# Local attention on four engines: other step orders, and other places for the next stage's first steps

## The chip, the cores and the metric

The kernel runs on one core of a Trainium2 chip. The core has TensorE (PE, matmuls and transposes), VectorE (DVE), ScalarE (ACT), GpSimd (POOL) and SyncE (SP, which only issues DMAs here). The time is the device time of one execution in microseconds, the median over runs.

## What is computed

The input is a stream `x` of 4 sequences of 512 tokens with 128 features. It goes through four residual blocks. The first is a cross-attention to 77 context rows, the third a second cross-attention, the fourth a mixture of 8 experts. The second block is the one that the change touches: six layers of local attention with a feed-forward part.

```python
def attn_layer(x, Wqkv, qs, ksc, Wo):
    qkv = x @ Wqkv                       # 16 heads of 64
    q, k, v = split into heads
    q = l2norm(q) * qs;  k = l2norm(k) * ksc
    q = q * cos * scale + rotate_half(q) * sin * scale
    k = k * cos / scale + rotate_half(k) * sin / scale
    out = local_attention(q, k, v)       # windows of 32, keys of own and previous window
    return out @ Wo
def ffn_layer(x, g, bln, W1, b1, W2, b2):
    xn = layernorm(x) * g + bln
    a, gate = split(xn @ W1 + b1)
    return a * gelu(gate) @ W2 + b2
for i in range(6):
    x = attn_layer(shift_tokens(x), ...) + x
    x = ffn_layer(shift_tokens(x), ...) + x
```

## The kernel before

The stage `windowed_layers` holds the second block. Its work is cut into 24 turns (`TURNS`: 6 layers times 4 sequences, turn j is layer j // 4 of sequence j % 4) and 96 slots (`SLOTS`: slot u is tile u % 4, of 128 tokens, in turn u // 4). Everything is float32 and the instruction streams are fully unrolled.

One slot goes through these steps. PE: `project` (u, 0 to 5), one matmul each, 0 and 1 for the queries, 2 and 3 for the keys, 4 and 5 for the values, into two PSUM banks in alternation; `heads_t` (u, 0 to 3), four transposes each, which turn the normed and rotated queries (0, 1) and keys (2, 3); `scores`, 8 matmuls for the mask and 128 small ones; `probs_t` (u, 0 and 1), transposes; `pv`, 128 small matmuls; `out`, 8 matmuls (16 PE instructions with their float32 passes). ACT: squares of `project` 0 to 3 and copies of 4 and 5 into `V` (both are its `project` step), `root` (logarithm and exponential for the norms), `heads_t`, `exp`, `probs_t`, `attended`. DVE: `mul` (u, 0 to 3, the rope products, which also empty the projection bank), `norms` (sums of squares), `soft` (maximum and subtraction), `share` (sum and reciprocal), `residual`. POOL: `clamp`, `add` (the two rope products), `rope` (four small Newton operations and the scaling by the inverse norm), `weigh` (probabilities by the reciprocal).

Per turn there is the feed-forward part: PE `back`, `norm_t`, `up` (0 to 5, on the projection banks), `down`; ACT `back`, `gelu`; DVE `stats`, `scale`, `hidden`, `down`; POOL `rstd`. `enter` and `leave` bring the stream in and out of this stage. With the first slot of a layer POOL computes the rope table of the layer (`table`, L799) just ahead of the first `clamp`, and DVE's `mul` waits for it. SP copies V shifted by 32 rows for each slot: after `v_done` of `project` 4 the lower half (L755), after that of `project` 5 and the landing of the lower half the upper one (L758); then, for u below 68, it fills a part of `sorted_rows` in HBM for a later stage (L777), and ahead of the next slot it copies the 32 rows that wrap (L752).

What runs when is written out by hand in four lists, `PE_TURN`, `ACT_TURN`, `DVE_TURN` and `POOL_TURN`: the steps of one turn, with the slot relative to the turn (-2 to 7) and the step's number. `steps` repeats a list for j from -2 to TURNS + 2 and leaves out slots that do not exist, so an engine's list may begin anywhere in the cycle; only the cyclic order counts. Each engine executes its list in order, with semaphore waits on the others. A step's PSUM bank for the shared kinds is dealt out in PE's order, in a ring of four (`homes`). The dictionary `FIRST` hangs the next stage's first steps (`f_...`, a part of the second cross-attention for the first sequence) behind named steps near the end.

Of the kernel before, what the change touches and what calls it, by code (L numbers as in the profile page):

```python
# [2479 lines left out]
```

## Time and profile before

| | us |
|---|---|
| median of 3 runs | 2054.53 |
| lowest and highest | 2050.99, 2066.19 |
| the profiled execution | 2048.87 |
| its span, first to last instruction | 2047.1 |
| mean granted clock of PE, share of full | 0.958 |

The stage of the change fills the span from about 113 to 1806 us, the first cross-attention stands ahead of it and the rest of the second one with the experts behind it. Durations below are of the one profiled execution; so a sum that is made from them is made against its 2048.87 us. In a group's row of the page "busy" is the union of its instructions, the mean is of one of them, and behind the bar stands the idle time of the engine just before them with what ended it. PE is the matmul queue, PEld the weight loads beside it; each PE instruction counted in the program is one load and one matmul.

### The profile page before, as it was taken

The page shows a single profiled execution, that of the slowest core. Times are in us where ns is not written, and L with a number is a line of the kernel's source. Part 1 is how long each engine was busy: PE and PEld are TensorE (multiplying, and loading weights), DVE is VectorE, ACT ScalarE, POOL GpSimd, SP SyncE. Part 2 cuts the span into 40 slices and gives each one's busy share as a digit, 9 for nine tenths or more (in the row PEclk, how much of TensorE's full clock was granted, in tenths as well). Part 3 has the DMA queues.
Part 4 walks back from the last instruction along what each step waited for, and adds up shares of the span by engine and source line. Part 5 has one row for each costly group of instructions (what it writes and reads, how often), then busy time and mean ns, then how long its engine had stood idle before and what let it go on. Part 6 is the DMA issues. An engine that isn't in the chain of part 4 may idle for free. (4 is left out here: it accounts for less than half of the span.)

```text
span 2047.1 us, 78950 instructions
## 1 busy us (share of the span) xinstructions
PE 1850.1 (90%) x32837; PEld 1300.6 (64%) x32837; DVE 1440.9 (70%) x2605; ACT 1135.4 (55%) x2379; POOL 1435.4 (70%) x1838
## 2 busy tenths in 40 slices
PE   4769999999999999999999989999999999789858
PEld 3636666666666666666666656666666676556648
DVE  2357778777777777787778867778777787445546
ACT  1135665566566566665566656566656665434425
POOL 1168888778888788788778877888778887412334
PEclk9779999999999999999999999999999999889969
DMA  3021131111311113111113111121111111030012
GB/s 98 0 40 50 47 96 55 42 43 49 101 47 43 49 47 94 50 49 47 46 47 100 51 43 44 34 82 35 27 34 31 37 31 33 10 95 1 22 34 69
DMA packets 60836, 99.93 MB, mean 49 GB/s; under 512 B 15847, under 2 KB 35064, under 8 KB 58642
## 3 DMA queue, kind: packets, MB, share of 16 engines
q1 hardware_dynamic: 58978, 91.72, 15.5%
q8 instruction: 262, 4.29, 0.9%
q0 software_dynamic: 1504, 3.17, 0.5%
q14 instruction: 92, 0.75, 0.1%
HBM read 44.50 MB, written 21.45 MB: 32 GB/s over the span
## 5 line engine op out<-in xcount | busy, mean ns | idle before, releaser
L1273 PE MATMUL b_bank_proj<-layer_weights,b_stream_t 128*128 128x512 f32 x1152 | 616.9, 635 | 21.0 <-DVE b_plain_moved L1069 17.5
L1069 DVE TENSOR_TENSOR b_plain_moved<-b_bank_proj,b_rope 128x1024 f32<-128x1024 f32 x384 | 468.9, 1222 | 210.3 <-ACT b_squares L903 179.2
L812 POOL TENSOR_TENSOR b_rotated<-b_plain_moved 128x1024 f32<-128x1024 f32 x192 | 452.5, 2357 | 42.6 <-DVE b_plain_moved L1069 42.6
L827 POOL TENSOR_TENSOR b_rotated<-b_rotated,b_inv_norm 128x1024 f32<-128x1024 f32 x192 | 365.2, 1902 | 15.4
L903 ACT ACTIVATE b_squares<-b_bank_proj 128x512 f32<-128x512 f32 x384 | 229.6, 598 | 110.2 <-PE b_bank_proj L1273 107.6
L832 POOL TENSOR_TENSOR b_probs<-b_probs,b_inv_sum 128x512 f32<-128x512 f32 x192 | 200.3, 1044 | 81.7 <-DVE b_inv_sum L1090 81.7
L1281 PEld LDWEIGHTS b_bank_shared<-const_tables,b_rotated 128*128 128x128 f32 x1536 | 187.7, 145 | 109.7 <-issue 103.5
L1273 PEld LDWEIGHTS b_bank_proj<-layer_weights,b_stream_t 128*128 128x128 f32 x1152 | 187.8, 195 | 108.7 <-issue 58.5
L1075 DVE TENSOR_REDUCE b_norm<-b_squares 128x16 f32<-128x1024 f32 x192 | 232.2, 1209 | 1.0 <-issue 0.2
L910 ACT ACTIVATE b_v<-b_bank_proj 128x512 f32<-128x512 f32 x192 | 114.5, 596 | 194.3 <-PE b_bank_proj L1273 194.3
L1281 PE MATMUL b_bank_shared<-const_tables,b_rotated 128*128 128x128 f32 x1536 | 210.8, 279 | 2.5 <-POOL b_rotated L827 2.4
L940 ACT ACTIVATE b_attended_t<-b_bank_shared 128x512 f32<-128x512 f32 x192 | 109.5, 596 | 168.5 <-PE b_bank_shared L1335 168.5
L1347 PEld LDWEIGHTS b_bank_shared<-b_attended_t,layer_weights 128*128 128x128 f32 x1536 | 184.5, 193 | 26.6 <-issue 25.8
L1347 PE MATMUL b_bank_shared<-b_attended_t,layer_weights 128*128 128x128 f32 x1536 | 188.3, 276 | 1.6 <-ACT b_attended_t L940 1.6
L1081 DVE TENSOR_REDUCE b_max<-b_bank_scores 128x8 f32<-128x512 f32 x192 | 131.6, 685 | 62.6 <-PE b_bank_scores L1306 62.2
L1306 PE MATMUL b_bank_scores<-b_k_t,b_q_t 64*32 64x64 f32 x12288 | 148.4, 225 | 27.6 <-issue 26.4
L1306 PEld LDWEIGHTS b_bank_scores<-b_k_t,b_q_t 64*32 64x32 f32 x12288 | 141.4, 105 | 38.4 <-issue 31.6
L924 ACT ACTIVATE b_k_t<-b_bank_shared 128x512 f32<-128x512 f32 x192 | 106.4, 594 | 91.4 <-PE b_bank_shared L1281 91.4
L1316 PEld LDWEIGHTS b_bank_shared<-const_tables,b_probs 128*128 128x128 f32 x768 | 95.2, 141 | 87.4 <-issue 86.8
L1335 PE MATMUL b_bank_shared<-b_probs_t,b_v 64*64 64x32 f32 x6144 | 118.5, 222 | 33.4 <-issue 33.1
L1378 PE MATMUL b_bank_proj<-b_normed_t,layer_weights 128*128 128x512 f32 (+1 forms) x288 | 141.3, 600 | 0.5 <-DVE b_normed_t L1119 0.5
L1087 DVE TENSOR_REDUCE b_sum<-b_probs 128x8 f32<-128x512 f32 x192 | 128.9, 671 | 15.5 <-ACT b_probs L930 15.3
(346 smaller groups left out, 2920.9 us busy)
## 6 DMA issues: line engine op xcount, KB each, us to landing
b_v_shifted<-b_v SPq DMA_DIRECT2D x192, 192.0 KB, 2.4
sorted_rows<-sorted_rows SPq DMA_DIRECT2D x66, 258.0 KB
layer_weights<-L_ffn_Wqkv SPq DMA_DIRECT2D x6, 1536.0 KB
b_v_shifted<-b_v SPq DMA_DIRECT2D x72, 128.0 KB, 3.1
layer_weights<-L_ffn_Wo SPq DMA_DIRECT2D x6, 512.0 KB
c_sorted_in<-sorted_rows SPq DMA_DIRECT2D x23, 129.0 KB, 2.0
layer_weights<-L_ffn_w SPq DMA_DIRECT2D x8, 256.0 KB, 6.1
c_w<-L_ffn_w SPq DMA_DIRECT2D x8, 256.0 KB, 5.9
```

Of the source, the lines that this page charges most:

```text
L812: nc.gpsimd.tensor_tensor(out=turned[:, k, :], in0=pm[:, k, 0, :], in1=pm[:, k, 1, :], op=ALU.add).then_inc(add_done, 1)
L827: nc.gpsimd.tensor_tensor(out=tk, in0=tk, in1=repeat_last(rn[:, k, :], DH), op=ALU.mult).then_inc(rope_done, 1)
L832: nc.gpsimd.tensor_tensor(out=p, in0=p, in1=repeat_last(share[:, b, :], LOOK), op=ALU.mult).then_inc(p_done, 1)
L903: nc.scalar.activation(squares[:, (c % 2) * 512:(c % 2) * 512 + 512], bk_proj[c % 2][:, :], ACT.Square).then_inc(sq_done, 1)
L1069: nc.vector.tensor_tensor(to, src.to_broadcast(shape), tab.to_broadcast(shape), ALU.mult).then_inc(mul_done, 1)
L1075: nc.vector.tensor_reduce(ss[:, k, :], squares[:, :].rearrange("p (a h c) -> p h a c", a=2, h=HEADS), AX.XY, ALU.add).then_inc(ss_done, 1)
L1081: nc.vector.tensor_reduce(top[:, b, :], s, AX.X, ALU.max).then_inc(max_done, 1)
L1273: nc.tensor.matmul(out, xs[:, b, t * P:(t + 1) * P], w, start=True, stop=True).then_inc(proj_full, 1)
L1281: last = nc.tensor.transpose(bank[:, n * P:(n + 1) * P], turned[:, g // 2, at:at + P], ident)
L1306: last = nc.tensor.matmul(bk_s[r][to, at:at + LOOK], qT[rows, u % 2, p, w, :], kT[rows, p, t * P + w * WIN:t * P + w * WIN + LOOK], start= ...
L1347: last = nc.tensor.matmul(bank[:, 0:P], weights(l, W_O + n * P, P), OT[:, u % 2, n, :], start=(n == 0), stop=(n == PAIRS - 1))
L1378: nc.tensor.matmul(bk_proj[c % 2][0:w, :], weights(l, W_UP + at, w), xnT[:, :], start=True, stop=True).then_inc(up_full, 1)
```

## The change

Only the four lists and `FIRST` change. Every list holds the same steps per turn as before, with a few of them counted from another turn (for example `leave` at -2 in place of -3), and in another order. In the cyclic order of PE: before, `down(-2)` stood behind `pv(-2)`, after it stands ahead of it; `probs_t(-1, 0)` moves ahead of `scores(0)`; `out(-2)` from ahead of `scores(0)` to behind `probs_t(-1, 1)`; `scores(1)` from behind `back(-1)` to ahead of it; `scores(2)` from behind the first four `up` to behind the first; `scores(3)` (written -1 before) from the middle of the projections of slot 4 to behind the last `up`; `heads_t(4, 0)` and `(4, 1)` (written 0) from behind `project(5, 0)` to ahead of `project(4, 5)`; `heads_t(3, 0)` and `(3, 1)` from behind `project(4, 2)` to ahead of it. On DVE `norms(4, 0)` goes ahead of `mul(4, 0)` (in the other slots it mostly keeps its place or moves by one), `soft` and `residual` steps move by a few places. On POOL `clamp`, `add` and `weigh` change places around the `rope` steps. On ACT `exp`, `attended`, `root` and `heads_t` steps move.

In `FIRST`, `f_weights` on PE goes from behind the last `out` to behind the last `back`; on DVE `f_stream` moves up behind a `share`, `f_normed` goes from behind the last `scale` to behind the last `stats`, `f_own` behind the second last `hidden`; on POOL `f_fill` and `f_rstd` hang behind `weigh` steps.

The lists of PE, DVE and POOL, and `FIRST`:

```diff
 PE_TURN = [
-    ("project", 0, 3), ("scores", -1, 0), ("project", 0, 4), ("probs_t", -2, 0), ("project", 0, 5), ("leave", -3, 0),
-    ("probs_t", -2, 1), ("project", 1, 0), ("heads_t", 0, 0), ("project", 1, 1), ("enter", 1, 0), ("heads_t", 0, 1),
-    ("pv", -2, 0), ("project", 1, 2), ("down", -2, 0), ("heads_t", 0, 2), ("heads_t", 0, 3), ("project", 1, 3),
-    ("project", 1, 4), ("out", -2, 0), ("scores", 0, 0), ("project", 1, 5), ("probs_t", -1, 0), ("project", 2, 0),
-    ("probs_t", -1, 1), ("project", 2, 1), ("heads_t", 1, 0), ("heads_t", 1, 1), ("pv", -1, 0), ("project", 2, 2),
-    ("project", 2, 3), ("out", -1, 0), ("heads_t", 1, 2), ("heads_t", 1, 3), ("project", 2, 4), ("back", -1, 0),
-    ("probs_t", 0, 0), ("scores", 1, 0), ("project", 2, 5), ("project", 3, 0), ("probs_t", 0, 1), ("project", 3, 1),
-    ("pv", 0, 0), ("project", 3, 2), ("heads_t", 2, 0), ("heads_t", 2, 1), ("project", 3, 3), ("norm_t", -1, 0),
-    ("out", 0, 0), ("up", -1, 0), ("heads_t", 2, 2), ("heads_t", 2, 3), ("up", -1, 1), ("probs_t", 1, 0),
-    ("up", -1, 2), ("up", -1, 3), ("scores", 2, 0), ("project", 3, 4), ("project", 3, 5), ("probs_t", 1, 1),
-    ("project", 4, 0), ("project", 4, 1), ("pv", 1, 0), ("project", 4, 2), ("heads_t", 3, 0), ("heads_t", 3, 1),
-    ("out", 1, 0), ("up", -1, 4), ("up", -1, 5), ("heads_t", 3, 2), ("heads_t", 3, 3),
+    ("heads_t", 0, 0), ("heads_t", 0, 1), ("project", 0, 5), ("probs_t", -2, 1), ("project", 1, 0), ("project", 1, 1),
+    ("down", -2, 0), ("project", 1, 2), ("pv", -2, 0), ("project", 1, 3), ("heads_t", 0, 2), ("heads_t", 0, 3),
+    ("probs_t", -1, 0), ("project", 1, 4), ("scores", 0, 0), ("project", 1, 5), ("heads_t", 1, 0), ("project", 2, 0),
+    ("project", 2, 1), ("heads_t", 1, 1), ("probs_t", -1, 1), ("out", -2, 0), ("project", 2, 2), ("enter", 1, 0),
+    ("pv", -1, 0), ("project", 2, 3), ("heads_t", 1, 2), ("heads_t", 1, 3), ("out", -1, 0), ("scores", 1, 0),
+    ("back", -1, 0), ("project", 2, 4), ("project", 2, 5), ("probs_t", 0, 0), ("probs_t", 0, 1), ("heads_t", 2, 0),
+    ("project", 3, 0), ("heads_t", 2, 1), ("project", 3, 1), ("pv", 0, 0), ("project", 3, 2), ("norm_t", -1, 0),
+    ("project", 3, 3), ("out", 0, 0), ("heads_t", 2, 2), ("heads_t", 2, 3), ("up", -1, 0), ("scores", 2, 0),
+    ("up", -1, 1), ("up", -1, 2), ("up", -1, 3), ("probs_t", 1, 0), ("project", 3, 4), ("project", 3, 5),
+    ("probs_t", 1, 1), ("project", 4, 0), ("project", 4, 1), ("pv", 1, 0), ("heads_t", 3, 0), ("heads_t", 3, 1),
+    ("project", 4, 2), ("out", 1, 0), ("heads_t", 3, 2), ("heads_t", 3, 3), ("up", -1, 4), ("up", -1, 5),
+    ("leave", -2, 0), ("scores", 3, 0), ("project", 4, 3), ("project", 4, 4), ("probs_t", 2, 0),
 ]
...
 DVE_TURN = [
-    ("soft", 2, 1), ("mul", 4, 0), ("norms", 4, 0), ("mul", 4, 1), ("mul", 4, 2), ("share", 2, 0), ("hidden", -1, 1),
-    ("hidden", -1, 2), ("share", 2, 1), ("residual", 1, 0), ("mul", 4, 3), ("norms", 4, 1), ("soft", 3, 0),
-    ("soft", 3, 1), ("mul", 5, 0), ("share", 3, 0), ("mul", 5, 1), ("norms", 5, 0), ("share", 3, 1), ("mul", 5, 2),
-    ("down", -1, 0), ("mul", 5, 3), ("norms", 5, 1), ("residual", 2, 0), ("soft", 4, 0), ("soft", 4, 1),
-    ("mul", 6, 0), ("mul", 6, 1), ("norms", 6, 0), ("share", 4, 0), ("share", 4, 1), ("mul", 6, 2),
-    ("residual", 3, 0), ("norms", 6, 1), ("mul", 6, 3), ("stats", 0, 0), ("soft", 5, 0), ("mul", 7, 0), ("mul", 7, 1),
-    ("norms", 7, 0), ("soft", 5, 1), ("mul", 7, 2), ("scale", 0, 0), ("share", 5, 0), ("mul", 7, 3), ("share", 5, 1),
-    ("norms", 7, 1), ("residual", 4, 0), ("hidden", 0, 0), ("soft", 6, 0),
+    ("share", 1, 0), ("mul", 3, 2), ("scale", -1, 0), ("mul", 3, 3), ("share", 1, 1), ("norms", 3, 1),
+    ("residual", 0, 0), ("hidden", -1, 0), ("soft", 2, 0), ("soft", 2, 1), ("norms", 4, 0), ("mul", 4, 0),
+    ("share", 2, 0), ("mul", 4, 1), ("mul", 4, 2), ("share", 2, 1), ("residual", 1, 0), ("hidden", -1, 1),
+    ("hidden", -1, 2), ("soft", 3, 0), ("mul", 4, 3), ("norms", 4, 1), ("share", 3, 0), ("soft", 3, 1), ("mul", 5, 0),
+    ("norms", 5, 0), ("mul", 5, 1), ("down", -1, 0), ("mul", 5, 2), ("share", 3, 1), ("mul", 5, 3), ("norms", 5, 1),
+    ("soft", 4, 0), ("soft", 4, 1), ("mul", 6, 0), ("norms", 6, 0), ("mul", 6, 1), ("share", 4, 0),
+    ("residual", 2, 0), ("mul", 6, 2), ("share", 4, 1), ("mul", 6, 3), ("norms", 6, 1), ("residual", 3, 0),
+    ("soft", 5, 0), ("stats", 0, 0), ("soft", 5, 1), ("mul", 7, 0), ("mul", 7, 1), ("norms", 7, 0),
 ]
...
 POOL_TURN = [
-    ("add", -1, 0), ("weigh", -3, 1), ("clamp", -1, 1), ("rope", -1, 0), ("add", -1, 1), ("clamp", 0, 0),
-    ("rope", -1, 1), ("add", 0, 0), ("weigh", -2, 0), ("weigh", -2, 1), ("rope", 0, 0), ("clamp", 0, 1),
-    ("add", 0, 1), ("rope", 0, 1), ("add", 1, 0), ("clamp", 1, 0), ("weigh", -1, 0), ("rope", 1, 0), ("weigh", -1, 1),
-    ("clamp", 1, 1), ("add", 1, 1), ("rope", 1, 1), ("add", 2, 0), ("clamp", 2, 0), ("weigh", 0, 0), ("rope", 2, 0),
-    ("clamp", 2, 1), ("weigh", 0, 1), ("add", 2, 1), ("rstd", -1, 0), ("clamp", 3, 0), ("rope", 2, 1),
-    ("weigh", 1, 0),
+    ("clamp", 5, 0), ("add", 5, 0), ("rope", 5, 0), ("weigh", 3, 1), ("clamp", 5, 1), ("add", 5, 1), ("rope", 5, 1),
+    ("clamp", 6, 0), ("add", 6, 0), ("weigh", 4, 0), ("rope", 6, 0), ("weigh", 4, 1), ("add", 6, 1), ("clamp", 6, 1),
+    ("rstd", 0, 0), ("rope", 6, 1), ("clamp", 7, 0), ("add", 7, 0), ("weigh", 5, 0), ("weigh", 5, 1), ("clamp", 7, 1),
+    ("rope", 7, 0), ("add", 7, 1), ("clamp", 8, 0), ("rope", 7, 1), ("weigh", 6, 0), ("add", 8, 0), ("rope", 8, 0),
+    ("weigh", 6, 1), ("add", 8, 1), ("clamp", 8, 1), ("weigh", 7, 0), ("rope", 8, 1),
 ]
...
 FIRST = {
-    "pe": {("out", SLOTS - 1, 0): ("f_weights",), ("norm_t", TURNS - 1, 0): ("f_contexts",),
+    "pe": {("back", TURNS - 1, 0): ("f_weights",), ("norm_t", TURNS - 1, 0): ("f_contexts",),
             ("up", TURNS - 1, 1): ("f_normed", "f_keys",), ("up", TURNS - 1, 3): ("f_queries",),
             ("up", TURNS - 1, 5): ("f_scores", "leave",), ("down", TURNS - 1, 0): ("f_counts",)},
     "act": {("back", TURNS - 1, 0): ("f_weights", "f_contexts",), ("gelu", TURNS - 1, 0): ("f_normed",),
             ("gelu", TURNS - 1, 2): ("f_keys", "f_queries", "f_scores", "leave", "f_counts",)},
-    "dve": {("residual", SLOTS - 2, 0): ("f_stream",), ("scale", TURNS - 1, 0): ("f_normed", "f_own",),
+    "dve": {("share", SLOTS - 2, 0): ("f_stream",), ("stats", TURNS - 1, 0): ("f_normed",), ("hidden", TURNS - 1, 1): ("f_own",),
             ("hidden", TURNS - 1, 2): ("f_best",), ("down", TURNS - 1, 0): ("f_counts",)},
-    "pool": {("rope", SLOTS - 4, 1): ("f_fill",), ("rstd", TURNS - 1, 0): ("f_rstd",)},
+    "pool": {("weigh", SLOTS - 6, 1): ("f_fill",), ("weigh", SLOTS - 2, 0): ("f_rstd",)},
 }
```

The list of ACT (80 steps) is left out. In its new order `project`, `heads_t` and `probs_t` keep the sequence that PE's new order gives them nearly throughout, with `exp(3, 1)` (written -1) behind `root(5, 0)` and the two `attended` of a slot close together.

## Rows read from the trace of the kernel before

**Rows 1.** The page of the profile: busy time of the engines; two DMA kinds; one issue.

```profile
PE 1850.1 (90%) x32837; PEld 1300.6 (64%) x32837; DVE 1440.9 (70%) x2605; ACT 1135.4 (55%) x2379; POOL 1435.4 (70%) x1838
...
q8 instruction: 262, 4.29, 0.9%
...
b_v_shifted<-b_v SPq DMA_DIRECT2D x192, 192.0 KB, 2.4
```

**Rows 2.** Windows, a turn without and one with a new layer: us, busy by engine, PEclk, DMA share, GB/s.

```profile
1119.40:1186.40 67.00, 63.95 (x1291) 43.95 (x1290) 53.26 (x79) 41.84 (x86) 56.55 (x71) 1.00 0.17 48
1186.40:1258.40 72.00, 65.74 (x1292) 45.02 (x1291) 53.31 (x79) 41.85 (x86) 57.62 (x74) 0.98 0.16 45
```

**Rows 3.** Waits over the whole span: engine, line, releaser: us in total, times, longest.

```profile
PE b_bank_shared L1335 <- issue: 39.4, 33, 2.1
...
PE b_bank_scores L1306 <- issue: 26.4, 32, 1.5
...
DVE b_plain_moved L1069 <- POOL b_rope L799: 23.9, 6, 5.3
```

**Rows 4.** Timeline of PE, turn of a new layer: start us, duration us, instructions.

```profile
1186.87 1.95 PE L1347 MATMUL b_bank_shared<-b_attended_t,layer_weights 128*128 128x128 f32 x16
1188.66 1.02 PE L1378 MATMUL b_bank_proj<-b_normed_t,layer_weights 128*128 128x512 f32 x2
1189.52 1.04 PE L1281 MATMUL b_bank_shared<-const_tables,b_rotated 128*128 128x128 f32 x8
...
1193.50 0.41 PE L1296 MATMUL b_bank_scores<-b_mask_bands,b_mask_rows 64*32 64x512 bf16 x8
...
1195.12 1.99 PE L1273 MATMUL b_bank_proj<-layer_weights,b_stream_t 128*128 128x512 f32 x4
```

**Rows 5.** Timeline, all engines, the first slot of a new layer.

```profile
1198.89 2.79 POOL L799 TENSOR_TENSOR b_rope<-const_tables,b_qk_scale 128x256 f32<-128x256 f32 x4
1199.19 1.13 PE L1335 MATMUL b_bank_shared<-b_probs_t,b_v_shifted 64*64 64x32 f32 x64
...
1202.99 2.07 PE L1273 MATMUL b_bank_proj<-layer_weights,b_stream_t 128*128 128x512 f32 x2 [1.73 <-DVE b_plain_moved L1069]
...
1204.35 0.22 POOL L817 TENSOR_TENSOR b_newton_half<-b_inv_norm_first 128x16 f32<-128x16 f32 x1
...
1205.54 1.90 POOL L827 TENSOR_TENSOR b_rotated<-b_rotated,b_inv_norm 128x1024 f32<-128x1024 f32 x1
```

**Rows 6.** The page, costliest groups: busy us, mean ns of one | idle before.

```profile
L1069 DVE TENSOR_TENSOR b_plain_moved<-b_bank_proj,b_rope 128x1024 f32<-128x1024 f32 x384 | 468.9, 1222 | 210.3 <-ACT b_squares L903 179.2
L812 POOL TENSOR_TENSOR b_rotated<-b_plain_moved 128x1024 f32<-128x1024 f32 x192 | 452.5, 2357 | 42.6 <-DVE b_plain_moved L1069 42.6
L827 POOL TENSOR_TENSOR b_rotated<-b_rotated,b_inv_norm 128x1024 f32<-128x1024 f32 x192 | 365.2, 1902 | 15.4
L903 ACT ACTIVATE b_squares<-b_bank_proj 128x512 f32<-128x512 f32 x384 | 229.6, 598 | 110.2 <-PE b_bank_proj L1273 107.6
L832 POOL TENSOR_TENSOR b_probs<-b_probs,b_inv_sum 128x512 f32<-128x512 f32 x192 | 200.3, 1044 | 81.7 <-DVE b_inv_sum L1090 81.7
...
L1075 DVE TENSOR_REDUCE b_norm<-b_squares 128x16 f32<-128x1024 f32 x192 | 232.2, 1209 | 1.0 <-issue 0.2
```

**Rows 7.** Timeline of PE, a gap inside a `scores` step.

```profile
1009.88 0.68 PE L1306 MATMUL b_bank_scores<-b_k_t,b_q_t 64*32 64x64 f32 x43 [1.05 <-issue]
```

**Rows 8.** Timeline, PE and the SP queue, a gap inside the `pv` step after `scores(1)`.

```profile
975.20 0.51 SPq L758 DMA_DIRECT2D b_v_shifted<-b_v  x1
...
976.74 1.14 PE L1335 MATMUL b_bank_shared<-b_probs_t,b_v_shifted 64*64 64x32 f32 x64
...
977.64 0.54 SPq L777 DMA_DIRECT2D sorted_rows<-sorted_rows  x1
...
980.31 0.81 PE L1335 MATMUL b_bank_shared<-b_probs_t,b_v 64*64 64x32 f32 x41 [2.09 <-issue]
```

**Rows 9.** Windows, the same stretch: us, busy by engine, PEclk, DMA share, GB/s.

```profile
976.20:977.40 1.20, 1.17 (x47) 0.69 (x48) 1.20 (x1) 0.98 (x3) 1.20 (x3) 1.00 0.57 164
```

More of the change, by code:

```diff
@@ L513 @@
-    ("exp", 0, 1), ("attended", -1, 0), ("attended", -1, 1), ("project", 2, 2), ("heads_t", 1, 1), ("root", 2, 0),
-    ("project", 2, 3), ("heads_t", 1, 2), ("heads_t", 1, 3), ("back", -1, 0), ("project", 2, 4), ("probs_t", 0, 0),
-    ("project", 2, 5), ("project", 3, 0), ("probs_t", 0, 1), ("project", 3, 1), ("root", 2, 1), ("attended", 0, 0),
-    ("exp", 1, 0), ("project", 3, 2), ("attended", 0, 1), ("project", 3, 3), ("exp", 1, 1), ("root", 3, 0),
-    ("heads_t", 2, 0), ("heads_t", 2, 1), ("gelu", -1, 0), ("gelu", -1, 1), ("heads_t", 2, 2), ("heads_t", 2, 3),
@@ L518 @@
-    ("gelu", -1, 2), ("probs_t", 1, 0), ("project", 3, 4), ("project", 3, 5), ("probs_t", 1, 1), ("project", 4, 0),
-    ("root", 3, 1), ("project", 4, 1), ("attended", 1, 0), ("attended", 1, 1), ("project", 4, 2), ("heads_t", 3, 0),
+    ("heads_t", 0, 1), ("probs_t", -2, 1), ("project", 1, 2), ("root", 1, 0), ("exp", -1, 1), ("attended", -2, 0),
+    ("project", 1, 3), ("heads_t", 0, 2), ("heads_t", 0, 3), ("project", 1, 4), ("attended", -2, 1),
+    ("probs_t", -1, 0), ("project", 1, 5), ("root", 1, 1), ("project", 2, 0), ("exp", 0, 0), ("project", 2, 1),
@@ new lines @@
+    ("heads_t", 1, 0), ("heads_t", 1, 1), ("probs_t", -1, 1), ("exp", 0, 1), ("root", 2, 0), ("project", 2, 2),
+    ("attended", -1, 0), ("attended", -1, 1), ("enter", 1, 0), ("project", 2, 3), ("heads_t", 1, 2),
+    ("heads_t", 1, 3), ("back", -1, 0), ("project", 2, 4), ("project", 2, 5), ("probs_t", 0, 0), ("exp", 1, 0),
+    ("probs_t", 0, 1), ("project", 3, 0), ("project", 3, 1), ("heads_t", 2, 0), ("root", 2, 1), ("heads_t", 2, 1),
+    ("attended", 0, 0), ("attended", 0, 1), ("project", 3, 2), ("project", 3, 3), ("exp", 1, 1), ("root", 3, 0),
@@ new lines @@
+    ("heads_t", 2, 2), ("heads_t", 2, 3), ("gelu", -1, 0), ("gelu", -1, 1), ("gelu", -1, 2), ("probs_t", 1, 0),
+    ("project", 3, 4), ("project", 3, 5), ("probs_t", 1, 1), ("root", 3, 1), ("project", 4, 0), ("project", 4, 1),
+    ("exp", 2, 0), ("exp", 2, 1), ("attended", 1, 0), ("attended", 1, 1), ("root", 4, 0), ("project", 4, 2),
+    ("heads_t", 3, 0), ("heads_t", 3, 1), ("heads_t", 3, 2), ("heads_t", 3, 3), ("project", 4, 3), ("project", 4, 4),
+    ("exp", 3, 0), ("leave", -2, 0), ("heads_t", 4, 0), ("probs_t", 2, 0), ("project", 4, 5), ("project", 5, 0),
@@ L520 @@
+    ("root", 4, 1), ("project", 5, 1),
 ]
 DVE_TURN = [
-    ("soft", 2, 1), ("mul", 4, 0), ("norms", 4, 0), ("mul", 4, 1), ("mul", 4, 2), ("share", 2, 0), ("hidden", -1, 1),
-    ("hidden", -1, 2), ("share", 2, 1), ("residual", 1, 0), ("mul", 4, 3), ("norms", 4, 1), ("soft", 3, 0),
-    ("soft", 3, 1), ("mul", 5, 0), ("share", 3, 0), ("mul", 5, 1), ("norms", 5, 0), ("share", 3, 1), ("mul", 5, 2),
-    ("down", -1, 0), ("mul", 5, 3), ("norms", 5, 1), ("residual", 2, 0), ("soft", 4, 0), ("soft", 4, 1),
```

6 lines of the change are left out of this document (removed).

## Prediction

> **What bounds the kernel.** I read the page first: TensorE (PE) is busy 1850.1 us, VectorE (DVE) 1440.9, GpSimd (POOL) 1435.4, ScalarE 1135.4 [rows 1]. Then windows cut at `norm_t`, one for each turn of the stage. A turn without a new layer lasts 67.0 us, with PE busy 63.95 and POOL 56.55; a turn in which a layer begins lasts 72.0, with PE at 65.74 and a lower granted clock [rows 2]. The change permutes the same steps, so PE's work stays and only what lies between its steps can move. The waits say what that is: 39.4 us inside `pv` and 26.4 inside `scores`, both "issue" (PE waits for nothing that the profile shows), and 23.9 us of DVE waiting for the rope table [rows 3].
>
> The "issue" gaps are instruction supply. The instruction queue moved 4.29 MB in 262 packets, 16.4 KB each; PE ran 2 x 32837 instructions and about a thousand waits, so a packet is some 256 of them [rows 1]. A `scores` step is 272 PE instructions in 1.62 us (1195.12 - 1193.50) [rows 4], a `pv` step 256 and a few waits in 3.80 - 1.73 = 2.07 us [rows 5]. Elsewhere PE is slow per instruction: `out` takes 32 in 1.79 us, a 512-wide projection 2 in some 0.9 (the `up` of rows 4 shows 0.86). So a block lasts long everywhere but in those two steps. They stop for 1.05 us [rows 7], and once for 2.09 [rows 8].
>
> **The change, part by part.** No step is added or removed. PE's step times without gaps, from rows 4 and 5: `project` and `up` 0.87, `heads_t` and `probs_t` 0.44, `scores` 1.62, `pv` 2.0, `out` 1.79, `down` 2.6 (three chunks of two `up`-sized matmuls).
>
> *A, start of a layer (5 times in the steady part).* Before: `project(4,0)`, `(4,1)`, `pv`, `project(4,2)`. POOL ends the table at 1201.68; DVE can only then do `mul(4,0)` (1.22 us), which empties the bank of `project(4,2)`; PE stands 1.73 us and then runs two matmuls in 2.07 where 1.02 is usual for the shape [rows 4, 5]. After: two `heads_t` (0.87) stand ahead of `project(4,2)`, and on DVE `norms(4,0)` goes ahead of `mul(4,0)`, filling the table's wait. If POOL starts the table as late as now, `mul(4,0)` ends 3.75 us after the `pv` begins and PE wants it at 2.9: the gap falls to about 0.87, 5 x 0.87 = 4.3 us. The slow clock behind it costs 1.05 us on that pair and some 0.6 on what follows; if three of five such spells go, 3 x 1.6 = 4.8. A is -9. Bounds: -4 (gap alone), -17 (gap and clock loss gone, 5 x 3.3).
>
> *B, tighter chains in every turn.* `norms` before `mul(4,0)` makes the bank of `project(4,2)` free 0.60 + 1.21 + 1.22 + some 0.1 = 3.15 us after `project(4,1)` [rows 6]; PE arrives after 2.0 + 0.87 = 2.88. That is 0.27 us a turn, hidden when PE stands in the `pv` between. Then `heads_t(4,0)`: behind `project(4,1)` stand on POOL the clamp, `rope(3,1)` (small steps 1205.54 - 1204.35 = 1.19, then 1.90), `weigh(2,0)` 1.04, `add(4,0)` 2.36, `rope(4,0)` 3.09 [rows 5, 6]; with the square 0.60, `norms` 1.21 and hand-overs that is 11.8 us. PE gets there after `pv`, 2 `heads_t`, `project`, `out`, 2 `heads_t`, 2 `up`, `scores`, 2 `project`, `probs_t` = 11.9 us. It is hidden by 0.1 us only. POOL is busy 56.55 of 67 us [rows 2], so its queue is nowhere far behind; what waits behind `rope(4,0)` is `weigh`, `add(4,1)`, `rope(4,1)`, whose reader `heads_t(4,2)` has 3 us to spare. Before, `project(4,1)` to `heads_t(4,0)` took 14.1 us by the same step times. The other shortened leads (`project(5,1)` to `heads_t(5,0)`, 15.4 to 11.0 us) have at least 1.6 us left by the same sum. I take +3 over 23 turns; bounds 0 (PE's own gaps cover it) and +12 (0.5 us a turn).
>
> *C, instruction supply.* Each fast step is as long as a block, so each holds about one block boundary in either order: 65 gaps in 192 fast steps [rows 3] stay about 65. What can change is their length. Before, `scores(1)` and `pv(0)` are 3.05 us apart, `scores(2)` and `pv(1)` 3.9, the others 4.3 or more; after, `pv(-2)` and `scores(0)` are 3.05 apart, `pv(-1)` and `scores(1)` 3.5, the others 5.7 or more. About even. The 2.09 us gap has one more thing in it: SyncE issued the upper half of V's shifted copy at 975.20, the DMA engines were 0.57 busy from 976.20 to 977.40, and `pv` began at 976.74 [rows 8, 9]; I read the gap as a block whose transfer stood behind V's. In the new order that copy still meets `pv(0)`: its lower half is issued by `project(2,4)`, 4.35 us ahead, and the upper one after its landing 2.4 us later [rows 1]. And `pv(-2)` and `pv(-1)`, 5.65 us behind `project(0,5)` and `project(1,5)` now, meet the next transfer, the filling of `sorted_rows` (L777), issued when V's copy has landed; this copy ends after 68 of the 96 slots, 17 turns. At a third of 34 steps (33 `pv` gaps in 96 [rows 3]) and 2.09 - 1.05 = 1.04 us, that is +12; my times for those transfers are good to half a microsecond, so I count half, +6, and -4 for the pairs moved apart. C is +2. Bounds: -18 (every gap in `pv` at 0.6 us in place of 1.2) and +22 (all collisions, and a spell of slow clock of 1.6 us behind six of them).
>
> *D, ends of the stage.* `f_weights` moves behind `back(23)`, `f_normed` ahead of `scale(23)`, `f_stream` and `f_rstd` earlier: all of it fills waits of the last turn's serial chain (`back`, statistics, `norm_t`, `up`, `down`), which no part of the change shortens. If that cover fails, a step of about a microsecond shows. At the head `norms(0,0)` fills DVE's first wait for the table (longest 5.3 us [rows 3]), but `heads_t(0,0)` now stands ahead of `project(0,5)` and `(1,0)`. I take 0; bounds -3 and +4.
>
> Sum: -9 + 3 + 2 + 0 = -4, against the profiled execution's 2048.9 us (span 2047.1 and 1.8 around it): 2045. The median of the runs shown, 2054.5, lies 5.7 above that execution and their lowest, 2051.0, 2 above; on the median's scale the same sum is about 2050. I give 2045.
>
> The Trainium skill, "Runtime: NRT & Kernel Launch", "Instruction fetch mechanics", says that an engine's instructions come in blocks of 16 KiB (256) through its own DMA queue, and that crossing a block is mostly hidden. The block size agrees with rows 1; the second half does not, by rows 7 and 8. By that page C would be 0 and the sum 2043.
>
> **Rivals.** *R1, the fast steps' gaps shrink.* The 65.8 us of rows 3 fall by a third to a half, since the widest-spaced order leaves the blocks time to arrive, and the clock spells behind the long gaps go too: -22 to -33, with A and B 2048.9 - 6 - 25 = 2018. For it: two of the pairs that are close now are 5.7 and 7.0 us apart afterwards. Against: every fast step still runs through a whole block in 1.6 to 2 us, and two other pairs are close. 27 in 100.
>
> *R2, the other side: the `sorted_rows` filling meets the fast steps.* Place: `pv(-2)` and `pv(-1)`, first 17 turns. Price: +12 for the gaps and 1.6 us of slow clock behind eight of them, 13: 2048.9 - 6 + 25 = 2068, and later turns without the filling are a microsecond shorter. It decides if L777's transfer is still running when the `pv` begins, that is if it is issued less than about 3 us before. Against: half a microsecond of drift parts them. 14 in 100. The Trainium skill, "DMA: Bandwidth & Descriptors", "Queues, rings and completion order", has each DMA engine take turns between queues packet by packet; by that a block waits for a packet and not for a transfer, and R2 costs nothing (2043). Rows 8 and 9 rather speak for a wait of a microsecond.
>
> *R3, POOL's chain becomes the bound.* If hand-overs cost 0.6 us more than I count, PE waits at every `heads_t(4,0)`: 23 x 0.6 = 14 over A, 2056; with the same at `heads_t(3,2)`, 2070. It decides when POOL's wait for `norms(4,0)` comes later than 2 us after `project(4,1)`. 9 in 100, half of it slower.
>
> *R4, the table is late anyway* and nothing else moves: 2048.9. This is inside my forecast's range.
>
> **The numbers.** Forecast with R4: 50 in 100, own range 2033 to 2060. About 1%, 20 us, is what a measurement of this kernel can tell from no change. Faster by over 1%: R1 and 1 more, 0.28. Slower: R2 and part of R3, 0.18. Within: 0.54. The range leaves out the far ends of R1 and of R2 with R3: 2022 to 2068.
>
> **What would show it.** A: DVE's wait for the table under 15 us in place of 23.9, PE's gap ahead of `project(4,2)` under 1 us, turns of a new layer near 69 us in place of 72. B: PE waits at L1281 for POOL L827, some tenths of a microsecond, where there were none. C: "issue" inside L1335 and L1306 at 55 to 80 us together, with the 2 us ones in `pv` steps whose start meets a transfer. R1: that sum under 45. R2: over 80, most of it in the first 17 turns. I am wrong in kind if turns without a new layer change by more than 1 us while those two sums stand still, or if the stage ends late.

## The result, and the profile after

The kernel after takes 1987.8 us (median of 4, 1985.6 to 1988.7), against 2053.7 for the kernel before beside it: 0.967 of its time, 95% interval 0.963 to 0.971. I had given 2045 (2022 to 2068), most of the chance for no measurable change. The direction had 28 in 100, and the time lies below the range. Two disturbed executions, one of the kernel before (2078.8 us, beside e5 to e8) and one of e7 (4524.6 us), are left out of every time and ratio below.

The page after, and windows of two stretches. The first row of windows is of the kernel after, from `norm_t` of turn 0 to that of turn 22; then turns 13 and 14, where a layer begins in the second (columns as in [rows 2]):

```profile
PE 1823.7 (92%) x32837; PEld 1278.3 (64%) x32837; DVE 1430.1 (72%) x2605; ACT 1138.5 (57%) x2379; POOL 1435.6 (72%) x1838
...
q8 instruction: 262, 4.29, 0.9%
```

```profile
218.60:1673.40 1454.80, 1416.55 (x28402) 968.25 (x28401) 1153.73 (x1717) 926.11 (x1896) 1221.70 (x1565) 0.99 0.18 53
```

```profile
1081.60:1150.20 68.60, 65.80 (x1291) 44.78 (x1290) 53.30 (x81) 42.20 (x87) 55.84 (x71) 0.98 0.17 47
1150.20:1214.20 64.00, 63.63 (x1291) 43.55 (x1290) 51.50 (x77) 41.99 (x87) 56.62 (x75) 1.00 0.19 54
```

The same stretch of turns in the kernel before:

```profile
226.40:1736.10 1509.70, 1435.67 (x28402) 986.02 (x28401) 1165.85 (x1717) 923.35 (x1895) 1223.68 (x1565) 0.98 0.18 51
```

These two long rows place 54.9 of the 63.3 us by which the span fell (2047.1 to 1983.8). PE idle fell from 1509.70 - 1435.67 = 74.0 us to 1454.80 - 1416.55 = 38.3 us. PE busy fell by 19.1 us with the same 28402 matmuls: that is the clock. In the clock's own record 14 spells at 1.2 GHz, 55 us in all, stand in that stretch before, and 5 spells, 17 us, after. Two more kernels below lie on the same line: with 37.5 us at 1.2 GHz (e10) PE is busy 1427.8 us there, with 6.8 us (e8) 1411.5, so a microsecond at 1.2 GHz costs half a microsecond. By kind of step (from the start of each PE instruction to the next one's) the stretch lost 31.4 us in `pv`, 11.4 in `scores`, 14.7 in `project` and 5.5 in `heads_t`, and `up` grew by 8.2. Ahead of the stretch 7.8 us went (226.4 to 218.6), behind it 0.6. By single turns the lower of the two kinds is now 64 us; the layer start of [rows 2] costs nothing of its own any more.

The waits after, to be held against [rows 3]:

```profile
PE b_bank_shared L1335 <- issue: 19.1, 21, 1.6
...
PE b_bank_scores L1306 <- issue: 15.0, 22, 1.9
...
PE b_bank_proj L1273 <- DVE b_plain_moved L1069: 9.7, 8, 3.1
...
PE b_bank_shared L1281 <- POOL b_rotated L827: 1.7, 1, 1.7
```

The "issue" sum inside the fast steps is 34.1 us in place of 65.8, in 43 gaps in place of 65. DVE's wait for the rope table is gone from the list.

### The profile page after: what moved, and what is told of

It is laid out like the page before. It is cut to its first block and busy times, and to the rows that moved or that the text cites. A ratio compares the mean times of both kernels' runs of the same rounds, so it can differ in the third digit from the quotient of the medians.

```text
span 1983.8 us, 78949 instructions
## 1 busy us (share of the span) xinstructions
PE 1823.7 (92%) x32837; PEld 1278.3 (64%) x32837; DVE 1430.1 (72%) x2605; ACT 1138.5 (57%) x2379; POOL 1435.6 (72%) x1838
## 5 line engine op out<-in xcount | busy, mean ns | idle before, releaser
L1273 PE MATMUL b_bank_proj<-layer_weights,b_stream_t 128*128 128x512 f32 x1152 | 591.6, 615 | 13.6 <-DVE b_plain_moved L1069 9.7
L1281 PEld LDWEIGHTS b_bank_shared<-const_tables,b_rotated 128*128 128x128 f32 x1536 | 180.6, 143 | 72.2 <-issue 67.4
L1335 PEld LDWEIGHTS b_bank_shared<-b_probs_t,b_v_shifted 64*64 64x64 f32 x6144 | 98.4, 134 | 71.9 <-issue 71.1
L1083 DVE TENSOR_TENSOR b_bank_scores<-b_bank_scores,b_max 128x512 f32<-128x512 f32 x192 | 134.3, 699 | 6.6
```

Source lines behind the costliest of these rows:

```text
L1083: nc.vector.tensor_tensor(s, s, repeat_last(top[:, b, :], LOOK), ALU.subtract).then_inc(sub_done, 1)
L1273: nc.tensor.matmul(out, xs[:, b, t * P:(t + 1) * P], w, start=True, stop=True).then_inc(proj_full, 1)
L1281: last = nc.tensor.transpose(bank[:, n * P:(n + 1) * P], turned[:, g // 2, at:at + P], ident)
```

## How a gap in a fast step comes about

The experiments below are read with this, so it stands first. PE's instructions come in 262 blocks before and after. The trace has 67146 records of PE's queue before (loads, matmuls, and 1472 of the queue itself, most of them semaphore instructions), which is 262.3 times 256. Counted over all of them, 59 of the 66 gaps of over 0.3 us in fast steps before stand at one place modulo 256, and 36 of 40 after; counted over loads and matmuls alone they stand at no common place. The transfer that ends a gap begins some 2.43 us before its end (2.30 to 2.75 for eight in ten of 937 gaps in the eighteen traces; a gap here is over 0.25 us lost from one matmul's start to the next). So a gap is 2.43 us less the time between the transfer's start and PE's arrival: where that time was above 2.4 us, 13 of 2553 boundaries in fast steps had a gap; where it was 1.2 to 1.8 us, all of 459.

What starts the transfer is seen in `pv(60)`, in the kernel after and in one in which `probs_t(0,1)` stands one step before `pv(0)` (e10 below). Block boundaries fall at almost the same instruction. First the kernel after: the last semaphore instruction of PE's queue ahead of the step (a source line's view: duration ns min/median/max, start), the step, and the DMA queue in the 0.1 us in which the block's packet begins.

```profile
L1327 PEldq EVENT_SEMAPHORE  x1: 51/51/51, 1145.1 to 1145.1; - x1
```

```profile
1146.26 1.14 PE L1335 MATMUL b_bank_shared<-b_probs_t,b_v_shifted 64*64 64x32 f32 x64
1147.21 0.87 PE L1335 MATMUL b_bank_shared<-b_probs_t,b_v 64*64 64x32 f32 x44
1148.79 0.54 PE L1335 MATMUL b_bank_shared<-b_probs_t,b_v 64*64 64x32 f32 x20 [0.71 <-issue]
```

```profile
q8 instruction: 1, 0.02, 79.1%
```

The packet begins between 1146.1 and 1146.2: 1.0 us behind the semaphore, 0.1 ahead of the step; PE goes on at 1148.79, 2.7 us after it began. In e10 ACT's copy ends just before the step:

```profile
1160.93 0.62 ACT L935 ACTIVATE b_probs_t<-b_bank_shared 128x512 f32<-128x512 f32 x1
```

```profile
L1327 PEldq EVENT_SEMAPHORE  x1: 51/51/51, 1161.6 to 1161.6; - x1
```

```profile
1161.75 1.13 PE L1335 MATMUL b_bank_shared<-b_probs_t,b_v_shifted 64*64 64x32 f32 x64 [0.57 <-ACT b_probs_t L935]
1162.68 0.90 PE L1335 MATMUL b_bank_shared<-b_probs_t,b_v 64*64 64x32 f32 x44
1165.66 0.54 PE L1335 MATMUL b_bank_shared<-b_probs_t,b_v 64*64 64x32 f32 x20 [2.08 <-issue]
```

Here the packet begins at 1163.2, and PE goes on 2.5 us later. PE's queue passed the semaphore 0.1 us ahead of the step in place of 1.1, and the gap is 2.08 us in place of 0.71. I call that distance, from the end of the queue's last semaphore record to the step's first matmul, the lead. Boundaries in the first 155 or so of a step's records are mostly fetched earlier: 13 of 2084 in the eighteen traces lost over 0.4 us, against 838 of 1487 behind them. Those are at risk. By place, over all slots (lead and transfer are medians, the transfer's start counted from the end of that semaphore; gaps are those that lost over 0.4 us, the mean is over all at risk):

| step, slot u mod 4 | kernel | steps ahead of it | lead us | transfer us | at risk | gaps | mean us |
|---|---|---|---|---|---|---|---|
| `pv` 0 | before | `probs_t`, `project` | 0.06 | 1.0 | 11 | 10 | 1.8 |
| `pv` 0 | after | `heads_t`, `project` | 1.15 | 1.0 | 9 | 6 | 0.6 |
| `pv` 0 | e10 | `probs_t`, `project` | 0.06 | 1.0 | 9 | 6 | 1.3 |
| `pv` 0 | e9 | `project`, `project` | 0.81 | 1.4 | 11 | 11 | 1.5 |
| `pv` 1 | before, after | `project`, `project` | 0.82 | 1.1, 1.0 | 8, 8 | 7, 6 | 1.1, 0.9 |
| `pv` 2 | before | `project`, `heads_t` | 1.69 | 1.0 | 9 | 4 | 0.4 |
| `pv` 2 | after | `down`, `project` | 1.61 | 1.8 | 10 | 8 | 1.0 |
| `pv` 2 | e8 | `down`, `project` | 1.61 | 1.0 | 10 | 0 | 0.1 |
| `pv` 3 | before | `heads_t`, `heads_t` | 0.83 | 0.8 | 10 | 6 | 0.7 |
| `pv` 3 | after | `out`, `project` | 1.09 | -1.8 | 9 | 0 | 0.0 |
| `pv` 3 | e6 | `probs_t`, `project` | 0.06 | 1.0 | 9 | 7 | 1.1 |
| `scores` 3 | before | `heads_t`, `project` | 1.01 | 1.0 | 12 | 10 | 1.1 |
| `scores` 3 | after | `up`, `up` | 2.21 | 1.1 | 13 | 2 | 0.2 |
| `scores` 3 | e5 | `out`, `project` | 2.57 | -0.4 | 12 | 1 | 0.0 |

So the transfer begins about 1.0 us behind the last semaphore at most places, later where it meets other transfers (`pv` 2 after, e9), earlier behind `out`. By lost time all gaps in fast steps together cost 72.3 us before and 43.2 after. `pv` 0 went from 20.1 to 5.7 us, `pv` 3 from 7.4 to 0, `scores` 3 from 12.9 to 2.0, `scores` 1 from 8.8 to 3.6; two places became worse, `pv` 2 (3.3 to 9.5) and `scores` 0 (2.0 to 9.5).

## The experiments

Ratios are to the kernel before beside each run. "Excess" is what a kind of step takes over the step times of the prediction, summed over the stretch of turns.

**e1, e2: halves of the change.** e1 has the lists of PE and ACT after and those of DVE and POOL before; e2 the reverse.

> PE's and ACT's lists (and their FIRST) of the kernel after, DVE's and POOL's of before. If the gain comes from PE's own order (fewer and shorter gaps inside scores and pv, fewer spells of slow clock), about 2005 us, with the issue gaps in L1335 and L1306 together near 35 us. If it comes from what DVE and POOL have ready in time, near 2045 or, since the lists no longer fit each other, slower than before.

> DVE's and POOL's lists of the kernel after under PE's and ACT's of before. If PE's order carries the gain, 2045 us (the table's wait only, 10 us) and the issue gaps still 60 to 70 us; if readiness carries it, 2010.

Measured: 2388.3 us (1.164, 1.160 to 1.168) and 2440.9 (1.191, 1.186 to 1.196), far outside every number expected. The largest wait of e1 is DVE standing for `out`:

```profile
DVE b_stream_t L1099 <- PE b_bank_shared L1348: 314.5, 48, 9.5
```

The lists fit in pairs of producer and consumer; no half carries a share of the gain that can be measured by itself.

**e3: `norms` first, in the kernel before.**

```diff
-    ("soft", 2, 1), ("mul", 4, 0), ("norms", 4, 0), ("mul", 4, 1),
+    ("soft", 2, 1), ("norms", 4, 0), ("mul", 4, 0), ("mul", 4, 1),
```

> Before, with norms(4,0) ahead of mul(4,0) on DVE, nothing else. My step A says that the gap at a layer's start is set by the end of mul(4,0) behind the table, and that is not moved by this alone: no gain at the layer starts, and PE has 2.0 us from project(4,1) to project(4,2) where the bank is free after 3.15: 1.1 us later in every turn, +15 to +25 us. If norms in the table's wait is what closed the gap of the new layer: -5 to -10.

Measured: 2060.9 (1.004, 1.003 to 1.006). PE's waits for the projection bank rose from 17.5 to 29.5 us:

```profile
PE b_bank_proj L1273 <- DVE b_plain_moved L1069: 29.5, 23, 3.1
```

The layer starts stay at 71 us and more: alone, that half of step A costs 0.5 us a turn where PE arrives early, as B said it might, and gains nothing, since the table is as late as before. The rise, 9 us, is under the 15 to 25 expected.

**e4, e12: where the blocks end.** e4 puts 33 no-operations ahead on PE. e12 makes the four transposes of the first `enter` nine times over, 64 PE records more.

> Before with 33 empty PE instructions ahead of everything, while PE waits for its first data: every boundary of a block falls 33 instructions elsewhere. If the after kernel's gaps are fewer by the luck of where the boundaries fall, this alone moves the issue gaps (65.8 us) by 15 us or more and the time by over 10. If the kind of step ahead of the fast steps decides, the gaps stay within 8 us and the time within 6 of before.

> The kernel before with the four transposes of the first enter step made nine times over (same result), 64 PE records more in front of the stage (32 transposes of one load and one matmul each). The instruction blocks then end 64 records earlier in every step of the stage, which the 33 no-operations did not bring about. If the shorter gaps of the kernel after were a matter of where blocks end, the gaps here change by a third or more (72 to under 50 us). If the order decides, they stay at 60 to 80 us and the time within 5 us of the kernel before plus some 4 us for the added transposes.

Measured: 2052.7 (1.001, 0.999 to 1.003) and 2056.2 (0.999, 0.996 to 1.002). In e4 the no-operations left no record and the gaps stand at the same steps' records as before, so it moved no boundary and tells nothing of them. e12 did move them, by 64 records, against the steps:

```profile
PE b_bank_shared L1335 <- issue: 44.2, 36, 2.3
PE b_bank_scores L1306 <- issue: 28.1, 31, 2.0
```

That is 72.3 us against the 65.8 of [rows 3]: 6.5 us more, where the change took 31.7 away. For this one shift a lucky position of the blocks is out as the cause.

**e5: `out` put ahead of a fast step.** The kernel before, with `out(1)` moved behind `up` 4 and 5 and two `heads_t`, so that `out` and `project` stand ahead of `scores(3)`.

> Before, with out(1) moved on PE from ahead of up(4), up(5) and the heads_t pair of slot 3 to behind them, so that out (32 PE instructions in 1.8 us) and one project stand directly ahead of scores(3). The block boundaries stay where they are in the stream. Theory run-ahead (a block is asked for while PE still works on a slow step with many instructions whose successors wait for nothing; then the fast step does not run dry): scores(3) loses most of its 12 us of gaps, 2053 becomes 2040 to 2045. Theory spacing or chance: scores(3) keeps its gaps, within 4 us of before.

Measured: 2061.2 (1.006, 1.003 to 1.009). `scores(3)` lost its gaps (excess 12.4 to -0.1 us), and their blocks' transfers mostly began ahead of the semaphore, as the table shows. But the time did not fall to the 2040 to 2045 expected, since a wait took their place, PE at `up` for the bank that `mul` empties, in every turn:

```profile
PE b_bank_proj L1378 <- DVE b_plain_moved L1069: 22.4, 22, 1.4
```

**e6: `out` taken away from a fast step.** The kernel after, with `out(-2)` three steps up, no longer behind `probs_t(-1,1)` and ahead of `pv(-1)`.

> After, with out(-2) on PE moved three steps up (ahead of heads_t(1,1) and probs_t(-1,1)), so that pv(-1), which has no gap in the after kernel, is preceded by heads_t, probs_t, project as the other pv steps are. Run-ahead: pv(-1) gets gaps of about 1.1 us in a third of the turns, +6 to +10 us. Spacing: nothing moves, within 3 us of after (1988).

Measured: 2040.4 (0.995, 0.993 to 0.997), 52 us over the kernel after. The gaps of `pv(-1)` came (0 to 7 of 9 at risk, 10.4 us), but they are the smaller part; PE now waits at its bank for the `residual` of the `out` moved, and the slow clock came back (51 us of 1.2 GHz):

```profile
PE b_bank_shared L1335 <- issue: 30.0, 28, 1.8
PE b_bank_shared L1335 <- DVE b_stream_t L1099: 29.1, 23, 1.3
```

So e6 changed two things. The queue stands at that wait until the step begins, which makes the lead 0.06 us; the gaps fit this, and say nothing of what `out` does by itself. `pv(83)`:

```profile
L1327 PEldq EVENT_SEMAPHORE  x1: 1333/1333/1333, 1574.7 to 1574.7; - x1
```

```profile
1576.12 1.14 PE L1335 MATMUL b_bank_shared<-b_probs_t,b_v_shifted 64*64 64x32 f32 x64 [1.31 <-DVE b_stream_t L1099]
```

**e7, e8: the upper half of V's copy later.** Before and after, one wait more on SP ahead of L758; what SP issues behind it, the filling of `sorted_rows` too, comes later.

```diff
                     sp.wait_ge(v2_low, 16 * (u + 1))
+                    wait(sp, pv_full, u - 1)
```

> Before, with SyncE holding the upper half of V's shifted copy (and the sorted_rows filling behind it) until pv of two slots earlier has ended, so that no copy of V is under way when pv(0) begins. Theory transfer (the 2 us gaps of pv(0) are a block's transfer that stands behind V's): pv(0) falls from 23 us of excess to about 12, and the spells of slow clock behind its long gaps go: 2053 becomes 2035 to 2043. If the transfers have nothing to do with it: within 4 us of before.

> After, with the same wait on SyncE. Transfer: the long gaps that are left (scores(0) up to 2.6 us, pv(-2) up to 1.8) shorten, -3 to -8 us on 1988, unless the copies meet scores(0) instead. Otherwise within 3 us.

Measured: 2064.2 (1.006, 1.003 to 1.009) and 1978.0 (0.967, 0.963 to 0.970; all four runs lie 5 us or more below the four of the kernel after, though the two ratios cannot tell them apart). In e7 the gaps of about 2 us in `pv(0)` are all there, and in the 2.5 us ahead of their blocks' transfers the DMA engines moved nothing else: [rows 8, 9] showed a coincidence. What e7 cost came in `scores(0)`, where the moved copies meet other transfers: five gaps of 2.2 to 2.7 us (12.2 us in all, 2.0 before), their blocks' transfers 3.9 to 4.3 us behind the semaphore with the DMA engines fully busy in the 2.5 us ahead.

```profile
PE b_bank_scores L1307 <- issue: 36.9, 35, 2.5
```

In e8 the gaps of `pv(2)` went. In the kernel after they were real collisions; `pv(58)` there, its SP queue, and the DMA share ahead of it (0.61), then in e8 (0.03):

```profile
1117.22 0.88 PE L1335 MATMUL b_bank_shared<-b_probs_t,b_v 64*64 64x32 f32 x48
1119.48 0.43 PE L1335 MATMUL b_bank_shared<-b_probs_t,b_v 64*64 64x32 f32 x16 [1.38 <-issue]
```

```profile
1114.09 0.54 SPq L777 DMA_DIRECT2D sorted_rows<-sorted_rows  x1
```

```profile
1114.70:1116.70 2.00, 2.00 (x33) 0.81 (x34) 2.00 (x3) 0.32 (x1) 1.92 (x3) 1.00 0.61 161
```

```profile
1107.50:1109.50 2.00, 2.00 (x35) 0.82 (x34) 2.00 (x3) 0.34 (x1) 1.92 (x3) 1.00 0.03 8
```

```profile
1109.05 1.14 PE L1336 MATMUL b_bank_shared<-b_probs_t,b_v_shifted 64*64 64x32 f32 x64
1110.01 1.32 PE L1336 MATMUL b_bank_shared<-b_probs_t,b_v 64*64 64x32 f32 x64
```

**e9, e10: the lead of `pv(0)` alone.** In e9, the kernel before, `probs_t(0,1)` goes one projection up on PE and ACT; in e10, the kernel after, it goes down to where it was.

```diff
-    ("project", 2, 5), ("project", 3, 0), ("probs_t", 0, 1), ("project", 3, 1), ("pv", 0, 0),
+    ("project", 2, 5), ("probs_t", 0, 1), ("project", 3, 0), ("project", 3, 1), ("pv", 0, 0),
```

> The kernel before, with probs_t(0,1) one step earlier on PE (ahead of project(3,0) in place of behind it) and ACT's copy of it likewise, so that two projections in place of one stand between it and pv(0). Run-ahead theory: PE's queue passes the last semaphore of pv(0) only when the copy of the probabilities is done, the next block's transfer starts about 1.0 us after that and its instructions are there 2.45 us later; in the kernel before, pv(0) is reached just as that wait ends (longest gaps, about 2.0 us, ten of them), and one projection more (0.87 us) gives the transfer that much: the 2 us gaps in pv(0) become about 1.2 us, gaps in all 72 to about 64 us, and with the slow spells behind them the time falls by 8 to 14 us (2038 to 2044). Rival (a block's transfer stands behind V's copy or the filling, or the gap is one per block whatever the order): no change in pv(0)'s gaps and in the time. A third possibility: the probabilities are not weighted yet a step earlier, PE waits at probs_t(0,1) for POOL, and the time rises by up to 0.87 us a turn, 20 us.

> The kernel after, with probs_t(0,1) put directly ahead of project(3,1) and pv(0), behind heads_t(2,0), project(3,0), heads_t(2,1), as in the kernel before (ACT's copy likewise). Run-ahead theory: pv(0)'s last wait then ends only as PE gets there, so the gaps in pv(0) grow from about 1.0 (6 of them) to 2.0 us and 6 to 10 occur, +8 to +14 us of gaps, slow spells return behind them (+3 to +8): 1998 to 2010. Rival (spacing of the fast steps alone decides, which this leaves as it is): within 2 us of the kernel after, 1988.

Measured: 2042.8 (0.992, 0.989 to 0.994) and 2023.3 (0.985, 0.980 to 0.990). e9: lead 0.06 to 0.81 us, the gaps fell from 2.0 to 1.5 us on average, less than the lead grew: their transfers began 1.4 us behind the semaphore in place of 1.0, with the DMA engines 0.6 to 0.7 busy in the microsecond ahead (that this delayed them is not shown). The time came as expected, but not for the reason given: `pv(0)` accounts for 3.3 us of it and all gaps together for 1; where the rest comes from is open. e10: lead 1.15 to 0.06, six gaps as before, from 0.95 to 1.96 us each. Its 35 us over the kernel after are more than these and more than expected: PE also stands at `pv` for the copy itself (14.1 us, 25 times), and the slow clock doubled (37.5 us at 1.2 GHz):

```profile
PE b_bank_shared L1335 <- ACT b_probs_t L935: 14.1, 25, 0.7
```

**e11: step A undone in the kernel after**, on PE and DVE.

```diff
-    ("project", 4, 1), ("pv", 1, 0), ("heads_t", 3, 0), ("heads_t", 3, 1), ("project", 4, 2),
+    ("project", 4, 1), ("pv", 1, 0), ("project", 4, 2), ("heads_t", 3, 0), ("heads_t", 3, 1),
...
-    ("norms", 4, 0), ("mul", 4, 0),
+    ("mul", 4, 0), ("norms", 4, 0),
```

> The kernel after with its answer to the late table undone: project(4,2) directly behind pv(1) and ahead of the two heads_t, and on DVE mul(4,0) ahead of norms(4,0), as before. If that part is worth what the trace says (five gaps of 1.7 us and the slow spells behind three of them), the time rises by 9 to 13 us, to 1997 to 2001, with gaps of about 1.7 us ahead of project(4,2) in the turns where a layer begins and nothing elsewhere. If the later waits absorb it, under 4 us.

Measured: 1992.7 (0.969, 0.964 to 0.974), 5 us over the kernel after, which the two ratios cannot tell from nothing (the kernel before took 2058.8 us beside e11 and 2053.7 beside the kernel after), and no gap of size ahead of `project(4,2)`. The table has become early. In the kernel after:

```profile
1161.89 2.81 POOL L799 TENSOR_TENSOR b_rope<-const_tables,b_qk_scale 128x256 f32<-128x256 f32 x4
...
1164.04 1.14 PE L1335 MATMUL b_bank_shared<-b_probs_t,b_v_shifted 64*64 64x32 f32 x64
...
1165.98 1.22 DVE L1069 TENSOR_TENSOR b_plain_moved<-b_bank_proj,b_rope 128x1024 f32<-128x1024 f32 x1
```

It ends 1164.70 - 1164.04 = 0.66 us into `pv(1)`, against 1201.68 - 1199.19 = 2.49 in [rows 4, 5]; `mul(4,0)` waits for its place behind `norms` and no longer for the table.

**e13, e14: the rule used forward.** On e8. e13 moves `probs_t(1,1)` a projection up on PE and ACT; e14 also moves `scores(2)` one `up` down.

> The kernel after with V's late upper half (1978 us) and with probs_t(1,1) one projection earlier on PE and ACT, so that three projections in place of two stand between it and pv(1). Run-ahead theory: pv(1) begins 1.85 us after the copy of its probabilities in place of 0.97, so its gaps of about 1.1 us (seven of them) shrink to some 0.3: pv(1) loses 5 to 7 us over its base time, the sum of gaps falls from 27 to about 21, the time to 1970 to 1974. Rival (a gap goes with each block whatever precedes): within 2 us of 1978.

> As the run above, and scores(2) one up later on PE, so that two up steps in place of one stand between the last transposes of its keys and it. Run-ahead theory: the copy of the keys lies 0.11 us ahead of scores(2) now and 0.97 us then; its gaps (9 us over base, some 8 of them) fall by half and the wait at its start goes, -4 to -6 us more: 1964 to 1970. If soft(2) or exp(2) then come too late for probs_t(2,0), PE waits there and the gain is lost: 1975 or more.

Measured: 1978.8 (0.966, 0.964 to 0.968) and 1970.6 (0.9605, 0.959 to 0.962). e13 failed, and says why: the copy of the probabilities now ends 1.78 us ahead of `pv(1)` in place of 0.97, but PE's queue passes the last semaphore 0.91 us ahead, as good as unchanged (0.82). Early data are not enough; the queue itself gets there only while the last projection runs. e14 is the fastest kernel of the study, 7 us under e8, but not for the reason given: `scores(2)` kept its gaps (excess 9.0 in e8, 7.8 here), and of the 10.2 us between the two profiled executions 5.4 are the excess of the `up` steps around it, 10.8 to 5.4 us, and 4.0 lie ahead of the stretch.

**e15, e16: POOL's list, and `FIRST`.** The kernel after with the old POOL list (and its entries in `FIRST`); with the whole old `FIRST`.

> The kernel after with the POOL list of before. If the new POOL list matters only by the early table, the gaps of 1.7 us ahead of project(4,2) come back in five turns and the time is 1995 to 2005. If its order fits the other lists in every slot, PE waits for POOL at heads_t in every turn (0.5 us or more, several times) and the time is above 2030.

> The kernel after with the FIRST dictionary of before: the next stage's first steps hang where they hung. If the new places are worth nothing, as the prediction had it, the time is within 3 us of the kernel after (1988); if they shorten the last turn or the next stage's start, it is 3 to 8 us more, and the time from the last norm_t to the end says so.

Measured: 2052.2 (1.001, 0.999 to 1.003) and 1987.4 (0.969, 0.967 to 0.970). With the old POOL list the whole gain is gone, but not by the table's gap, which stays away (it ends 1.1 us or less into `pv` at four of the five layer starts, 1.3 at the fifth): PE waits in every turn at `out` and `heads_t`.

```profile
PE b_bank_shared L1348 <- ACT b_attended_t L941: 18.2, 23, 1.3
...
PE b_bank_shared L1282 <- POOL b_rotated L828: 13.6, 28, 1.0
```

Its stretch ahead of turn 0 is 230.5 us long, so the 7.8 us there go with POOL's old list in place. The old `FIRST` changes nothing.

## Why the prediction was wrong

*What bounds the kernel* held: PE's gaps of instruction supply and the slow clock behind them were the thing to watch, and the change moved nothing else of size.

*A, the layer start*: right in kind, wrong in its premise. "If POOL starts the table as late as now" failed; it ends 1.8 us earlier against PE. So all of the gap went, not half of it: 11.9 us of gaps ahead of `project` in the stretch became 0.7. The term was also too small in kind. Over its 22 turns the five with a layer start lasted 73.0 us on average before and the others 67.4; after, both last 66.1. So layer starts gave 5 x (73.0 - 67.4) = 28 us, where I had -9 and -17 as the far bound: seven of the 14 slow spells stood in those turns, four of them at the wait for the table and three at gaps in `pv`, and I had priced three; so a part of the 28 us belongs to C. The other 27 us of the stretch are 1.2 us in every turn. e11 shows that the reordering that I priced is not what did it: undone, it costs 5 us or nothing.

*B, tighter chains*: +3 expected. The chain at `heads_t(4,0)` has one wait for POOL in the kernel after (1.7 us), and PE's waits for the projection bank fell (17.5 to 9.7 us). e3 shows such a wait in the old surroundings, 0.5 us a turn without the two `heads_t` ahead; in the new ones it is covered.

*C, instruction supply* is the step that failed, by its sentence "65 gaps in 192 fast steps stay about 65". A fast step does hold a boundary in either order (the block size that the prediction took from [rows 1] stands); whether PE stops there depends on when the block's transfer began: with the new leads, and in spite of the two places that now meet other transfers, 43 gaps are left. The numbers were in the trace: 11 boundaries at risk gave ten gaps of 2.0 us in `pv(0)`, and nine gave four of 0.4 to 0.9 us in `pv(2)`. I read the gap's length as spacing between fast steps and as collisions, and did not look at the queue's own records ahead of the step. I gave +2; "issue" fell by 31.7 us. e10 shows it most directly: the old lead alone brings the 2.0 us gaps back. And the sum priced the clock for three spells only (4.8 us): nine fewer, 37.5 us less at 1.2 GHz, were worth 19.1 us of PE's busy time.

*The collision of C and R2*: half right. `pv(-2)` (slot 2 mod 4) does meet the `sorted_rows` filling (e8 against the kernel after: excess 9.8 to 1.8 us), in the direction and near the size of the +6; `pv(-1)` does not, with `out` ahead of it. What the prediction did not name is `scores(0)`, 7.5 us worse, its long gaps behind 2.5 us of DMA shares of 0.7 to 1.0. The reading of [rows 8, 9] on which this stood was wrong (e7). The Trainium skill, "DMA: Bandwidth & Descriptors", "Queues, rings and completion order", has each DMA engine take turns between queues packet by packet, from which I concluded that a block waits for a packet only. The trace speaks against that conclusion: in `pv(58)` the block began 0.9 us into the step in place of 0.5 ahead of it.

*R1* named the right effect, gaps falling by a third to half and the clock spells with them; its 2018 left out the 7.8 us ahead of the stage, the rest of A, and most of the clock. Its reason, wider spacing, is not what the runs show: e10 changes the gaps with the spacing kept. *D* held (e16).

*Left open*: why `out` ahead of a fast step brings the transfer 2.4 to 3.4 us ahead of it although the lead at its semaphore is only 1.1 us (table, `pv` 3); which instruction asks for the block there; where e9's gain comes from; and how the 7.8 us ahead of turn 0 divide. One shift of the boundaries (e12) was tried, and only in the kernel before.

## What to carry to other kernels

Where short instructions run through a block in less time than the block takes to come, ask of each such step when the engine's queue gets past its last semaphore, not only how long the step is; a slow step of many instructions directly ahead (`out` here), with the data ready before it, can hide the whole transfer (e5). Orders of several engines are one object: the one list taken out alone (POOL's) cost as much as the set had gained, and two mixed pairs far more. And a gap costs more than its length where the clock falls behind it.
